# A selective scan on Trainium2: which operand of the column directions' copies takes the 64-word steps

## The reference, cut to what matters

```python
xc = silu(conv3x3(xa))
x_flat  = xc.reshape(Bn, Din, L)                                # row by row
x_trans = jnp.transpose(xc, (0, 1, 3, 2)).reshape(Bn, Din, L)   # column by column
x_hwwh = jnp.stack([x_flat, x_trans], axis=1)
xs = jnp.concatenate([x_hwwh, jnp.flip(x_hwwh, axis=-1)], axis=1)   # 4 directions
x_dbl = jnp.einsum('bkdl,kcd->bkcl', xs, x_proj_weight)         # dt rows, B, C
delta = softplus(dt_proj(dts) + bias)
def step(h, inp):                                               # along L
    dA = jnp.exp(d_l[..., None] * A)
    dBu = d_l[..., None] * B_l[:, :, None, :] * u_l[..., None]
    h = dA * h + dBu
    y = jnp.sum(h * C_l[:, :, None, :], axis=-1)
y = out_y[:, 0] + inv_y[:, 0] + wh_y + invwh_y                  # turned back to rows
```

## Time and profile before

| | us |
|---|---|
| median of the runs | 28435.44 |
| profiled execution | 28430.92 |
| its span | 28429.4 |
| PE busy | 25357.2 (89%) |
| DVE busy | 23856.0 (84%) |
| POOL busy | 22128.3 (78%) |
| ACT busy | 20735.5 (73%) |

### The profile page before, as it was taken

One profiled execution on the slowest core, in us unless ns is written; L12 is line 12 of the kernel. 1 busy time (PEld: TensorE's weight loads), 2 busy tenths in 40 slices (PEclk: granted clock), 3 DMA queues, 4 the chain that ended last, 5 costly groups with the idle time before them and its releaser, 6 DMA issues. The chain is left out here.

```text
span 28429.4 us, 291694 instructions
## 1 busy us (share of the span) xinstructions
PE 25357.2 (89%) x80480; PEld 11869.3 (42%) x80480; DVE 23856.0 (84%) x23376; ACT 20735.5 (73%) x38376; POOL 22128.3 (78%) x9798
## 2 busy tenths in 40 slices
PE   8899888998889988899888998889988899888998
PEld 3444334443344433444334443344433444334443
DVE  6799867998679986799867998679986799867998
ACT  4788647886478864788647886478864788647886
POOL 3799737997379973799737997379973799737997
PEclk8999989999899998999989999899998999989999
DMA  0111101111011110111101111011110111101111
GB/s 8 51 63 64 45 8 51 63 64 45 8 51 63 63 46 8 51 63 63 46 8 51 63 63 46 8 51 63 64 45 8 51 63 64 45 8 51 63 64 45
DMA packets 833671, 1309.75 MB, mean 46 GB/s; under 512 B 224897, under 2 KB 242177, under 8 KB 828929
## 3 DMA queue, kind: packets, MB, share of 16 engines
q1 hardware_dynamic: 832000, 1290.45, 14.6%
HBM read 1223.00 MB, written 67.11 MB: 45 GB/s over the span
## 5 line engine op out<-in xcount | busy, mean ns | idle before, releaser
L1592 PE MATMUL ps<-arena,ident 128*128 128x512 f32 x24576 | 11670.0, 601 | 50.9 <-DVE arena L1419 50.8
L1407 DVE TENSOR_TENSOR_SCAN arena<-ps,arena 128x512 f32<-128x512 f32 x6144 | 7492.6, 1261 | 329.5 <-issue 208.0
L1407 DVE TENSOR_TENSOR_SCAN arena<-arena,ps 128x512 f32<-128x512 f32 x6144 | 7413.5, 1257 | 121.7 <-ACT arena L1786 101.9
L1960 POOL TENSOR_TENSOR arena<-arena 128x1536 f32<-128x1536 f32 x2048 | 7067.8, 3457 | 146.2 <-DVE arena L1407 144.6
L1592 PEld LDWEIGHTS ps<-arena,ident 128*128 128x128 f32 x24576 | 4349.8, 192 | 4544.5 <-issue 4240.7
L1970 POOL TENSOR_TENSOR arena<-arena 128x1536 f32<-128x1536 f32 x1728 | 5971.4, 3463 | 52.8 <-ACT arena L1806 52.8
L1797 ACT ACTIVATE scaled<-arena,cols 128x384 f32<-128x384 f32 x8192 | 4711.4, 605 | 1032.5 <-PE ps L1560 1025.5
L1786 ACT ACTIVATE ps<-arena 128x512 f32<-128x512 f32 x6144 | 4123.6, 684 | 602.2 <-DVE arena L1407 592.6
L1786 ACT ACTIVATE arena<-arena 128x512 f32<-128x512 f32 x6144 | 4251.2, 716 | 100.1 <-PE ps L1592 99.0
L1560 PE MATMUL ps<-ident,scaled 128*128 128x128 f32 x24576 | 3612.6, 277 | 590.3 <-DVE arena L1407 420.1
L1560 PEld LDWEIGHTS ps<-ident,scaled 128*128 128x128 f32 x24576 | 2854.6, 141 | 3050.1 <-DVE arena L1407 1583.7
(11 more groups left out here) (187 smaller groups left out, 32595.1 us busy)
## 6 DMA issues: line engine op xcount, KB each, us to landing
arena<-rows SPq DMA_DIRECT2D x3776, 256.0 KB, 3.2
spare<-rows SPq DMA_DIRECT2D x576, 256.0 KB, 3.4
arena<-x SPq DMA_DIRECT2D x16, 1536.0 KB, 13.0
x<-arena SPq DMA_DIRECT2D x16, 1536.0 KB, 10.7
arena<-x SPq DMA_DIRECT2D x64, 384.0 KB, 8.7
out<-arena SPq DMA_DIRECT2D x64, 384.0 KB, 3.0
rows<-xd SPq DMA_DIRECT2D x256, 64.0 KB, 2.7
arena<-L_conv_fc_w SPq DMA_DIRECT2D x16, 576.0 KB, 5.2
```

The costliest lines, as they stand in the source:

```text
L1407: nc.vector.tensor_tensor_scan(flip(states(b, n, t)), flip(decays), flip(adds), carry[:, k, N2 * n + t:N2 * n + t + 1], ALU.mult, ALU.add) ...
L1592: nc.tensor.matmul(m.ps[:, t, :], m.ident[:, :], states(b, n, t), start=False, stop=(n == SUMS[t][-1])).then_inc(at[Y_MM[t]], 1)
L1960: nc.gpsimd.tensor_tensor(three(dbu[:, no % DB, :]), du[:, b % 2, :, :], each, ALU.mult).then_inc(at["db_ready"], 1)
```

## The change

In column blocks, the image side of the four instructions was read or written column by column: 64 words with steps of 64, eight times. The block's own side (`du` and `delta` in SBUF, the PSUM bank) was one run of 512 words. Now both views go row by row: the image side is 64 runs of eight neighbouring words, and the block's own side takes steps of 64 words from one element to the next. What is computed for which pixel and where it is stored stay the same. Row blocks are untouched.

```diff
         if k % 2 == 0:
             return v[:, t, i * T:(i + 1) * T]
         wide = T // H
-        return v.rearrange("p t (h w) -> p t w h", w=W)[:, t, i * wide:(i + 1) * wide, :]
+        return v.rearrange("p t (h w) -> p t h w", w=W)[:, t, :, i * wide:(i + 1) * wide]
 
     def shaped(b, v):
-        return v if b // NT % 2 == 0 else v.rearrange("p (w h) -> p w h", h=H)
+
+        return v if b // NT % 2 == 0 else v.rearrange("p (w h) -> p h w", h=H)
```

## The result

The changed kernel takes 28326.72 us (median of seven runs) against 28426.75 for the kernel before (median of its seven): ratio 0.9965, 95% interval [0.9953, 0.9976]. That is 100 us less, beyond the 57 us that I had called measurable. The profiled execution takes 28326.27 us, its span 28324.7. One of the seven runs was slow (32375 us, at a mean granted clock of 0.743 where the others have 0.94), and the ratio is of the others.

A forecast was written before the change was run, and what follows sets the result against it. It took DVE, held up by ACT's strided copies helped by PE, as the limit and POOL as second. Column blocks falling from 72.46 to 71.65 us, 120 x 0.81 = 97 us, gave 28338 us, range 28285 to 28520.

The forecast's parts named there:

- the first gap: DVE's 0.88 us wait before column-block scans at 1702.37, blamed on ACT's late decay(b, 5, 1); to shrink to about 0.15.
- The rule that a price lies "beside DVE's": In column blocks, PE's 5.2 us of possible record savings would not move the forecast by itself beyond 0.27 us.
- PE's records: rows_of and take_old, 12 records per column block, writing PSUM with steps: 592 ns (free) to 1026, neither end preferred.
- The copy: give_y on ACT, three per column block, reading PSUM with steps: 650 ns taken, between bounds of 585 and 1065.
- `du`: POOL's product, three per column block: 1.54 us taken, the strided write fitting into POOL's pace of 2.5 ns an element.
- POOL's path: POOL's time for a column block without its wait: 71.43 us, the floor while du stays at 1.54.
- The 1.03 us wait: POOL's wait for DVE at line 1987 in a column block, taken as its one real wait: 72.46 - 1.03 = 71.43 us.
- the rivals on POOL: du's strided write costs: in part, at 1.80 us 28407 (chance 0.23); or POOL bounds, kernel slower, 28486 to 29015 (0.12).
- The clock: If PE gets 5.2 us back, every second column block may lose 1 us to a lower granted clock: mean 71.84.
- The sum: Column block 71.65 us, the middle of 71.84 and 71.43; 0.81 us gained in 120 blocks, 97 us.

The follow-up runs named there:

- The copies alone: Changed kernel with only the copies of give_y on the new views; rows_of, take_old and du on the old ones: 28416.9 us, ratio 0.9997 to the kernel before.
- the matmuls alone: Changed kernel with only rows_of and take_old on the new views; give_y and du on the old ones: 28338.6 us, ratio 0.9969 to the kernel before.
- `turn_back` moved: Kernel before, all views old, with turn_back(b, 5, 0) moved ahead of add_up(b, 1, 0) on TensorE: 28405.6 us, ratio 0.9994.
- The filler: Changed kernel plus one float32 matmul (two records, 0.86 us) per block, just ahead of take_old(b, 2), filling idle time before delta_of(ahead, 1): 28227.7 us.
- the late filler: Changed kernel plus a float32 matmul of the same size per block, ahead of rows_of(ahead, 0), at the end of a block: 28349.4 us.

## Why the prediction was right, and where it was not

The number was close (28338 for 28327, 97 us of gain for 100), but the step that named the cause was wrong, and that the sum still met the time was partly luck.

*The cause of the first gap: wrong.* I wrote: "So the first DVE gap is ACT's strided copies, helped by PE." The copies alone gain nothing, the matmuls alone gain all but 12 us. In the row the group x3 at 1702.37 holds `scan(b, 5, 0)` to `scan(b, 5, 2)`; I took the first of them for `scan(b, 5, 1)` since the row names ACT. What it waited for stands in the timeline of PE in the kernel before, which I had not put beside ACT's:

```profile
1671.15 0.66 PE L1560 MATMUL ps<-ident,scaled 128*128 128x128 f32 x4 [0.35 <-DVE arena L1407]
...
1699.10 1.88 PE L1583 MATMUL ps<-arena,ident 128*128 128x512 f32 x2
1700.80 1.04 PE L1592 MATMUL ps<-arena,ident 128*128 128x512 f32 x2
1701.67 0.60 PE L1560 MATMUL ps<-ident,scaled 128*128 128x128 f32 x4
...
1706.73 1.12 PE L1530 MATMUL ps<-xd,arena 12*128 12x512 f32 x2
1707.78 2.84 PE L1592 MATMUL ps<-arena,ident 128*128 128x512 f32 x6
...
1711.61 0.65 PE L1560 MATMUL ps<-ident,scaled 128*128 128x128 f32 x4 [0.33 <-DVE arena L1407]
```

`turn_back(b, 5, 0)` runs from 1701.67 to 1702.27, and the scan starts at 1702.37. ACT's decay ended at 1702.29, 0.02 us later, and so got the name. PE has no gap between the first and the last row: from 1671.15 it is back to back through `delta_of(ahead, 1)` at 1706.73 and `add_up(b, 0, 0)` at 1707.78 to 1711. The same three calls in the changed kernel, with the gap that the shorter records leave:

```profile
1698.83 0.63 PE L1561 MATMUL ps<-ident,scaled 128*128 128x128 f32 x4
...
1704.93 1.09 PE L1531 MATMUL ps<-xd,arena 12*128 12x512 f32 x2 [0.95 <-DVE sp_e L1440]
1705.95 2.84 PE L1593 MATMUL ps<-arena,ident 128*128 128x512 f32 x6
```

The rule that a price lies "beside DVE's" failed with it: I had said of the 5.2 us of the records that "Neither moves the forecast by itself: beyond 0.27 us, PE's time lies beside DVE's." In column blocks PE, without a gap from well ahead of `rows_of` (1679.16) to `add_up(b, 0, 0)` (1707.78), set the pace. The first DVE gap was its sign, as the runs with the matmuls alone and with `turn_back` moved show. The second gap has another root: it stands in row blocks too (0.82 us) and goes only when the add is moved ahead of `delta_of(ahead, 1)`, which itself waits for DVE.

*PE's records: inside the bounds, at the free end.* I carried 592 and 1026 and preferred neither. They take 592 and 610. The Trainium skill's statement ("SBUF — State Buffer", section "Door 1: The DMA port swizzle") that any non-contiguous PSUM pattern slows matmuls down significantly does not hold for these float32 matmuls: with 64-word steps in the write, a record takes 592 ns, as without. No run here tries another type.

*The copy: 650 ns forecast, 585 measured, the free end of its bounds, and without effect on the blocks.* My reason, that a read need not fetch and put back anything, is not shown by any run.

*`du`: right.* 1.54 forecast, 1.52 measured, and the write costs next to nothing (some 20 ns), as the argument on the pace said; that the pace is the reason, no run shows. But its consequence was wrong: I set POOL's path at 71.43 us for "All else is back to back". The column blocks run at 71.27 in the changed kernel and at 71.0 to 71.1 where POOL is the bound. The 1.03 us wait was not all of POOL's slack; it had 0.3 to 0.4 us more, of which one further wait of 0.2 us for DVE stands in the view of POOL's waits in a column block of the kernel before (1687.4 to 1759.8 us):

```profile
POOL arena L1960 <- DVE arena L1407: 0.2, 1, 0.2
```

With the write at some 20 ns the rivals on POOL fall.

*The clock: right, and now shown.* I expected falls in every second column block if PE got its time back, a mean of 71.84, and took 71.65 between that and 71.43. They take 71.27 or 72.25 us, 40 of 104 the longer, a mean of 71.65. The filler takes all of them away and with them 99 us, about as much as the change gained.

*The sum.* PE did get its time back, so my own figure for that case was 71.84 us. The measured 71.65 lies under it for two reasons of like size: POOL's path was 0.16 us too dear, and the longer blocks are 40 of 104 and not half. My middle of 71.84 and 71.43, taken because I couldn't choose, falls on the same number. The column blocks give 104 x 0.82 = 85 us; another 12 us come from the row blocks, which I had called unchanged, with 12 fewer longer ones. Why these fell is open. With the cause wrong, the agreement is partly luck: had PE's writes cost 1026, the forecast of 28338 would have stood in the text and the kernel would have stayed near 28427, as the run with the copies alone did.

## What to carry to other kernels

When a wait has several semaphores, put the timelines of all engines side by side at that moment and compare ends, before naming a cause; a group x3 starts with its first instruction, not with the one that the named releaser would fit. An engine that runs without a gap up to the place where another waits is a bound there, even if its busy share over the whole kernel says nothing of it, and reordering ahead of the last call that is waited for doesn't help. When work is taken off TensorE, look where it will stand idle and what stands behind that place: moving one call into the hole gave 248 us, 2.5 times what the cheaper records gave. Of these the filler alone, which only keeps the clock up, gives 99; the rest is DVE no longer waiting for that call.

## What the runs showed of the hardware that I had not expected

- 64-word steps are free for a float32 matmul's write to PSUM (592 ns) and for ScalarE's read from PSUM (585), and dear for TensorE's read from SBUF (1026) and ScalarE's write to SBUF (1065).
- On GpSimd one strided read of two costs some 260 ns on 512 elements, whichever operand it is (1528 and 1537 against 1269); a strided write costs some 20 (1290).
- 0.95 us of idle time at one place comes with a fall of the granted clock in more than every third block (76 of 208 full blocks of the changed kernel); 0.83 us at another, 47 us later, with none once the first was filled. Ahead of the first place TensorE is also idle for 0.41, 0.19 and 0.28 us within 15 us. Why the one place and not the other was not settled. Nor was the count in row blocks, each with idle time at the first place: 48 of 104 in the kernel before, 36 in the changed one, 24 with `turn_back` moved, 50 with the late filler.
